# First attention of a ViT tower: norms of queries and keys by four 32-column tiles, one ScalarE copy and a selection matrix

## The reference

```python
q = split_heads(tokens @ Wq, HEADS)            # HEADS, DK, DV = 16, 16, 64
kv = split_heads(tokens @ Wkv, HEADS)
k, v = (kv[..., :DK], kv[..., DK:])
q, k, v = (l2norm(q), l2norm(k), l2norm(v))    # t / max(norm(t), 1e-12)
sim = jnp.einsum('bhid,bhjd->bhij', q, k)
attn = jnp.square(jax.nn.relu(sim))
out = jnp.einsum('bhij,bhjd->bhid', attn, v)
out = tanh_norm(out)                           # tanh(norm) * t / norm
```

## Time and profile before

| what | value |
|---|---|
| median of 3 runs | 3127.56 us (3121.09 to 3130.24) |
| the profiled execution: time, span | 3139.85 us, 3138.1 us |
| mean granted TensorE clock over the span | 0.963 |
| TensorE matmul, busy over the span | 2907.1 us (93%) |
| TensorE weight load, busy over the span | 2217.3 us (71%) |
| VectorE, busy over the span | 2098.8 us (67%) |
| ScalarE, busy over the span | 1442.7 us (46%) |
| GpSimd, busy over the span | 1157.0 us (37%) |

### The profile page before, as it was taken

How to read it: one execution, slowest core, us unless ns; L and a number is a source line. 1 busy time by engine, 2 the same in 40 slices (tenths; PEclk the granted TensorE clock), 3 DMA queues, 4 the chain that set the end, 5 groups by cost and what they waited for, 6 DMA issues and landing times. The chain is left out here.

```text
span 3138.1 us, 66657 instructions
## 1 busy us (share of the span) xinstructions
PE 2907.1 (93%) x21548; PEld 2217.3 (71%) x21549; DVE 2098.8 (67%) x5372; ACT 1442.7 (46%) x2948; POOL 1157.0 (37%) x966
## 2 busy tenths in 40 slices
PE   3899999999999999999966999999999972999998
PEld 1677777777777777777744666666766652999997
DVE  4577677677677777777734777777777855444444
ACT  0444544545545545445422555555555533444443
POOL 3324434434434334334321233333233324444443
PEclk7899999999999999999987999999999985999999
DMA  3424424424424424324302111111111101554544
GB/s 83 96 70 92 107 66 95 107 62 98 102 62 104 98 66 104 94 70 104 87 22 51 49 47 53 43 42 52 45 54 47 44 33 44 77 76 76 77 77 69
DMA packets 161126, 223.12 MB, mean 71 GB/s; under 512 B 30305, under 2 KB 125730, under 8 KB 161074
## 3 DMA queue, kind: packets, MB, share of 16 engines
q1 hardware_dynamic: 135138, 187.50, 23.9%
q0 software_dynamic: 25936, 34.95, 7.2%
HBM read 125.26 MB, written 97.08 MB: 71 GB/s over the span
## 5 line engine op out<-in xcount | busy, mean ns | idle before, releaser
L66 POOL TENSOR_TENSOR vrn<-vsm,inv_root 128x16 f32<-128x16 f32 x64 | 243.8, 3809 | 285.8 <-DVE vsm L836 285.8
L665 ACT ACTIVATE R<-psA 128x1024 f32<-128x1024 f32 x256 | 262.4, 1025 | 168.4 <-PE psA L1150 164.2
L857 DVE TENSOR_TENSOR PR<-R 128x1024 f32<-128x1024 f32 x256 | 321.3, 1255 | 0.0
L2512 POOL DMA_INDIRECT out_rows<-e_y,e_dest x137 | 213.7, 1560 | 289.8 <-DMA out_rows<-e_y,e_dest 182.2
L1904 DVE TENSOR_REDUCE m_nm<-psC 128x4 f32<-128x1028 f32 (+1 forms) x256 | 239.0, 956 | 72.0 <-PE psC L2177 71.4
L1165 PE MATMUL psA<-PR,V 128*64 128x258 f32 x2048 | 283.4, 398 | 0.0
L670 ACT ACTIVATE oTs<-psA 128x258 f32<-128x258 f32 x256 | 99.1, 387 | 358.1 <-PE psA L1165 352.3
L1783 ACT ACTIVATE m_PT<-psC 128x770 f32<-128x770 f32 x256 | 194.0, 810 | 137.3 <-PE psC L2205 137.3
L1210 PE MATMUL psA<-wout,OT 128*128 128x256 f32 x1024 | 244.6, 382 | 0.4 <-DVE OT L899 0.4
L1698 POOL DMA_INDIRECT xg<-tn,idx x124 | 124.5, 1004 | 318.6 <-DMA xg<-tn,idx 186.6
L1210 PEld LDWEIGHTS psA<-wout,OT 128*128 128x128 f32 x1024 | 188.7, 191 | 24.6 <-DVE OT L899 0.7
(11 more groups left out here) (417 smaller groups left out, 7633.0 us busy)
## 6 DMA issues: line engine op xcount, KB each, us to landing
ks<-kparts SPq DMA_DIRECT2D x256, 128.0 KB, 3.3
qs<-qparts SPq DMA_DIRECT2D x256, 128.0 KB, 3.8
e_x<-xg SPq DMA_DIRECT2D x143, 129.0 KB
xraw<-in_x SPq DMA_DIRECT2D x66, 256.0 KB
qparts<-qh SPq DMA_DIRECT2D x128, 128.0 KB, 2.4
kparts<-kh SPq DMA_DIRECT2D x64, 128.0 KB, 2.5
kparts<-kl SPq DMA_DIRECT2D x64, 128.0 KB, 2.4
qparts<-ql SPq DMA_DIRECT2D x64, 128.0 KB, 2.4
```

Of the source, the lines that this page charges most:

```text
L66: return pool.tensor_tensor(out, x, e.to_broadcast(list(out.shape)), ALU.pow)
L665: act.activation(R[:, p % 2].rearrange("p a t n -> p t a n"), ps[:, 0:2, :].rearrange("p t (a n) -> p t a n", a=2), ACT.Relu).then_inc(rel ...
L857: dve.tensor_tensor(PR[:, p % 2, :, :, 0:L], R[:, p % 2], R[:, p % 2], ALU.mult).then_inc(prob_done, 1)
L2512: pool.indirect_dma_start(out, bass.IndirectOffsetOnAxis(ap=dest[:, b % XD:b % XD + 1], axis=0), y[:, b % XD], None, compute_op=ALU.add).t ...
```

## The change

`key_sums` and `query_sums` are taken out. In their place `row_norms` multiplies with the indicator (now 32 columns, 24 of them zero) as the stationary operand and the squares as the moving one, into four tiles of 32 output rows, for both halves of the queries and of the keys. ScalarE copies the 128x256 result to SBUF (`norm_rows`), and `turn_norms` turns it with the selection matrix `sel32` into 32 columns for each half of the tokens. `query_norms` on VectorE moves up to stand right behind `key_norms`.

```diff
+            dve.memset(v.ind8[:, 8:32], 0.0)
+            dve.tensor_copy(v.sel32[:].rearrange("p (g m) -> p g m", g=4),
+                            v.ident[:].rearrange("p (g r) -> p g r", g=4)[:, :, 0:8])
...
+            def norm_rows(j):                       # ScalarE
+                act.wait_ge(norms_summed, j + 1)
+                act.activation(nsums[:], ps[:, BCLS, 0:L], ACT.Copy).then_inc(norms_copied, 1)
...
             def sample (ScalarE)
                     values(j, 1)
+                    norm_rows(j)
                 take_outputs(i, d, 5)
...
             def key_norms(j):                       # VectorE; query_norms likewise
-                dve.wait_ge(kn_done, j + 1)
+                dve.wait_ge(norms_turned, j + 1)
...
             def sample (VectorE)
                     key_norms(j)
+                    query_norms(j, e)
                     tokens(j + 1)
                     value_sums(j, 2)
                     value_sums(j, 3)
                     value_lift(j, 1)
                     value_rows(j, e, 0)
-                    query_norms(j, e)
                     value_rows(j, e, 1)
...
             def mixer_keys(j, t):                   # TensorE
+                if t == 0:
+                    need(pe, racl_done, j)
...
+            def row_norms(j):
+                pe.wait_ge(k_sq, j + 1)
+                pe.wait_ge(q_sq, j + 1)
+                for w, sq in enumerate((qsq, ksq)):
                     for c in range(2):
-                        col = at + 16 * t + 8 * c
-                        last = pe.matmul(ps[:, BCLS, col:col + 8], sq[:, c, t * P:(t + 1) * P], v.ind8[:], start=True,
-                                         stop=True, skip_group_check=True)
+                        g = 2 * w + c
+                        last = pe.matmul(ps[32 * g:32 * g + 32, BCLS, 0:L], v.ind8[:], sq[:, c, :], start=True, stop=True,
+                                         skip_group_check=True)
+                last.then_inc(norms_summed, 1)
+
+            def turn_norms(j):
+                pe.wait_ge(norms_copied, j + 1)
+                for t in range(LT):
+                    col = NORMS + 32 * t
+                    last = pe.matmul(ps[:, BCLS, col:col + 32], nsums[:, t * P:(t + 1) * P], v.sel32[:], start=True,
+                                     stop=True, skip_group_check=True)
+                last.then_inc(norms_turned, 1)
 
             def class_products(j):
-                pe.wait_ge(k_lift, j + 1)
+                pe.wait_ge(q_lift, j + 1)
...
             def sample (TensorE)
                     project_values(j, 1)
+                    row_norms(j)
                 attend(i, d, 5)
                 sim(i, 7)
                 if more:
-                    key_sums(j)
+                    turn_norms(j)
                     project_values(j, 2)
                     project_values(j, 3)
                     class_products(j)
                 attend(i, d, 6)
-                if more:
-                    query_sums(j)
                 attend(i, d, 7)
```

More of the change, by code:

```diff
@@ L416, in mixer_and_attention @@
         osums = sbuf(nc, ctx, "osums", [P, L])
+        nsums = sbuf(nc, ctx, "nsums", [P, L])
         ssb = sbuf(nc, ctx, "ssb", [P, 2, LT, HEADS])
@@ L804, in second_norm, with norms @@
                                       ALU.mult).then_inc(xn_done, 1)
+            def norms(w):
+                return ps[:, BCLS, NORMS:NORMS + 64].rearrange("p (t w g) -> p w t g", t=LT, w=2)[:, w]
             def key_norms(j):
-                dve.wait_ge(kn_done, j + 1)
-                dve.tensor_scalar(km[:], ps[:, BCLS, KN:KN + 32].rearrange("p (t g) -> p t g", t=LT), L2_EPS ** 2, None,
+                dve.wait_ge(norms_turned, j + 1)
+                dve.tensor_scalar(km[:], norms(1), L2_EPS ** 2, None,
                                   ALU.max).then_inc(k_lift, 1)
@@ L844, in query_norms @@
             def query_norms(j, e):
-                dve.wait_ge(qn_done, j + 1)
-                dve.tensor_scalar(qm[:], ps[:, BCLS, QN:QN + 32].rearrange("p (t g) -> p t g", t=LT), L2_EPS ** 2, None,
+                dve.wait_ge(norms_turned, j + 1)
+                dve.tensor_scalar(qm[:], norms(0), L2_EPS ** 2, None,
                                   ALU.max).then_inc(q_lift, 1)
@@ L1112, in project_values @@
                 last.then_inc(v_done, 1)
-            def norm_sums(sq, at):
-                for t in range(LT):
-                    for c in range(2):
-                        col = at + 16 * t + 8 * c
-                        last = pe.matmul(ps[:, BCLS, col:col + 8], sq[:, c, t * P:(t + 1) * P], v.ind8[:], start=True,
-                                         stop=True, skip_group_check=True)
[L1120 to L1124, removed]
+            def row_norms(j):
+                pe.wait_ge(k_sq, j + 1)
+                pe.wait_ge(q_sq, j + 1)
+                for w, sq in enumerate((qsq, ksq)):
+                    for c in range(2):
+                        g = 2 * w + c
[4 more added lines that the diff above has]
+                pe.wait_ge(norms_copied, j + 1)
+                for t in range(LT):
+                    col = NORMS + 32 * t
+                    last = pe.matmul(ps[:, BCLS, col:col + 32], nsums[:, t * P:(t + 1) * P], v.sel32[:], start=True,
+                                     stop=True, skip_group_check=True)
+                last.then_inc(norms_turned, 1)
             def class_products(j):
-                pe.wait_ge(k_lift, j + 1)
+                pe.wait_ge(q_lift, j + 1)
                 for k in range(KT):
@@ L1135, in class_products @@
                 last.then_inc(cls_done, 1)
[L1137 to L1140, removed]
             def sim(i, p):
@@ L2674, in first_weights @@
     v.biasr = sbuf(nc, ctx, "biasr", [P, 768], BF16)
-    v.ind8 = sbuf(nc, ctx, "ind8", [P, 8])
+    v.ind8 = sbuf(nc, ctx, "ind8", [P, 32])
+    v.sel32 = sbuf(nc, ctx, "sel32", [P, 32])
     v.sel8 = sbuf(nc, ctx, "sel8", [P, 8])
```

12 lines of the change are left out of this document (6 added, 6 removed).

## The result

The changed kernel takes 3138.83 us (median of 9 runs, 3136.29 to 3147.97) against 3128.1 us for the kernel before in the same series (9 runs, 3121.09 to 3138.68). The ratio is 1.0035, with a 95% interval from 1.0024 to 1.0047: 0.35% slower, 10.7 us by the medians. The forecast was 8.4 us more.

The account below looks back on a forecast made before the run. A loop through TensorE's work to project_values(j, 3) and a GpSimd chain was taken to bound the kernel. 31 x 0.30 = +9.3, -1.2 for DMA waits, +0.3 for constants: +8.4 us on 3127.56, 3136.0 us; range 3122 to 3144.

Parts of the forecast that it names:

- The loop: First attend, TensorE to project_values(j, 3), square, last sum, GpSimd root, class parts, prob, next first attend: 47.28 us per turn.
- the 30 waits of VectorE for `acl`: At 30 of 31 sample turns VectorE waits for GpSimd's acl before the first prob; read as sign that TensorE doesn't bound.
- TensorE inside the loop: Down to project_values(j, 3): row_norms 0.70 plus turn_norms 0.46 minus key_sums 0.90, +0.26 us per sample (0.23 to 0.32).
- the upper bound of 0.76: row_norms ahead of attend 5: 0.67 us, up to 0.76 if the matmul behind pays 0.09; 0.70 taken.
- 0.30 us: Growth taken per turn: VectorE delays the last value sum by 0.22 to 0.44 us, TensorE by 0.23 to 0.32; larger decides.
- Rival C: VectorE's moved query_norms decides: 0.36 to 0.50 us per turn, +10 to +15 us, around 3140; chance 0.24.
- A: The forecast itself: loop longer by 0.23 to 0.36 us, +6 to +10 us, 3133 to 3138; chance 0.56.
- The covers: ScalarE's copy ends before turn_norms is reached; class_products gets q_lift about when TensorE arrives, and lies outside the loop.
- Where the removed work went: TensorE's stall grows from 0.35 to about 1.3 us, split between sim(i+1, 0) for the DMA and the first attend.
- samples that wait for a late landing: Six later samples wait for the layout DMA anyway, partly covering the longer loop: at most 1.8 us, taken as -1.2.
- B: TensorE bounds the loop after all: all 0.64 us per sample comes back, -19.8 us, 3107.7; chance 0.12.
- D: The layout DMA lands later too: each further 0.1 us costs 3.1 us; with 0.3 us +18 us, 3145; chance 0.08.

Follow-up runs that it names:

- e2: Changed kernel with the four instructions of turn_norms issued twice, 0.43 us more TensorE work inside the loop; ratio 1.0074 to the kernel before.
- e3: Changed kernel with the eight query instructions of class_products issued twice, 0.89 us more TensorE work outside the loop; ratio 1.0041 to the kernel before.
- e4: Kernel before with query_sums cut from eight instructions to two, 0.66 us less TensorE work behind project_values(j, 3); ratio 0.9997.
- e1: Changed kernel run again without any edit; ratio 1.0042 to the kernel before.
- e10: Changed kernel with value chain taken forward, key_norms and query_norms ahead of value_sums(j, 3), each part's store started once written; 3102.21 us, ratio 0.9893 to the kernel before.
- e5: Changed kernel with query_norms behind value_lift(j, 1) on VectorE and class_products behind attend 6 on TensorE; ratio 1.0031 to the kernel before.
- e11: e10 with the old norm_sums for keys and queries instead of four tiles, copy and turn; 3120.18 us, ratio 0.9948 to the kernel before.
- e7: Changed kernel with row_norms behind project_values(j, 2), turn_norms behind project_values(j, 3), class_products behind attend 6, copy and VectorE reordered; ratio 0.9981 to the kernel before.
- e8: Changed kernel with value projections and sums taken forward, query_norms behind prob 7; ratio 0.998 to the kernel before.

## Why the prediction was right

**The loop.** The step on which all rests, that the turn of a sample is set by TensorE's work down to `project_values(j, 3)` and then by a chain over GpSimd, held. e2 and e3 show both sides of it: 13 us of work inside cost 12.1, 28 us outside cost 0.3 in the 31 turns. e4 shows the outer side in the kernel before. In all 31 turns of the kernel before, of the changed one and of e1 to e4, the last value sum starts 0.03 us behind its square.

One of the signs I had read it from proves less than I took it for, the 30 waits of VectorE for `acl`. e10 has the same row, though the turn there is set by TensorE:

```profile
DVE PR L873 <- POOL acl L582: 15.7, 30, 0.6
```

What tells the two apart is the time from `sim` to `attend`. Its shortest at this place is 0.65 us, not the 0.56 of another pair, so the stall in the kernel before was about 0.26 us, not 0.35.

**TensorE inside the loop.** `turn_norms` costs 856.03 - 855.66 = 0.37 us and 0.08 more on the instruction behind (0.31 to the next instead of 0.23), as forecast. `row_norms` was sized at 0.70 and costs 0.77. Its body takes the forecast 0.57 us (853.18 to 853.75), its entry 0.09 (two instructions of line 1125 take 0.55 instead of 2 x 0.23). The rest is the step behind the group, which I had priced at 0.09 in the upper bound of 0.76 and then left out of the 0.70: line 1176 takes 0.32 us to line 1181 (853.75 to 854.07), where in the kernel before the same pair stands 0.21 us apart:

```profile
848.53 0.28 PE L1160 MATMUL psA<-pcl,vcls 80*128 80x258 f32 x1
848.74 1.09 PE L1165 MATMUL psA<-PR,V 128*64 128x258 f32 x8
...
855.66 0.36 PE L1160 MATMUL psA<-pcl,vcls 80*128 80x258 f32 x1
...
855.96 1.09 PE L1165 MATMUL psA<-PR,V 128*64 128x258 f32 x8
```

The second pair of rows, also of the kernel before, stands behind `class_products`, which uses no 32-column tiles, and takes 0.30 us as well; so this step is no price of leaving the tiles. With 0.77 the sum is 0.77 + 0.45 - 0.90 = +0.32 us instead of +0.26; the row for the root says +0.37. The 0.05 that are left I can't attribute to one place: in the medians over the turns they come in steps of 0.01 to 0.02 us at instructions that are the same in both kernels.

**VectorE.** I took 0.30 us by arguing with both engines at once. The runs show that TensorE's part alone decides: the last sum starts 0.03 us behind its square before, after and in e5. Key and query norms together take 0.92 us (858.13 to 859.05), not 0.98, and the sums follow each other after 0.72 us, so VectorE comes just in time. Rival C is excluded, narrowly, and by these rows alone: the time itself, 10.7 us more, lies just above the 6 to 10 us of A, within the 10 to 15 of C.

**The covers.** ScalarE's copy (0.42 us, from 854.26 to 854.68) ended a microsecond before `turn_norms` at 855.66. `class_products` waits 0.17 us on average for `q_lift` (5.1 us, 30 times), outside the loop, as said.

**Where the removed work went.** The stall was forecast to grow to 1.3 us, split between the DMA and the chain. In the sample shown it is 0.24 us at `sim(i+1, 0)` and 821.85 - 820.27 - 0.56 = 1.02 us before `attend`, 1.26 together. Counted from 0.65 us instead of 0.56, this and the forecast are both 0.09 less.

**The sum.** 31 x 0.37 = 11.5 us, and the 31 turns grew by 9.3. I had taken off 1.2 us for samples that wait for a late landing; the traces show something else in that place. In 27 turns the growth is 10.1 us, 0.37 each. The first turn grew by 1.5 (46.00 to 47.52 us). Three turns got shorter, by 2.3 us together: the second, which had a late landing before (48.29 to 47.76), and the 13th and the 30th, which took 48.60 us each before because the clock was halved for 3.4 us in them. So the 8.1 us forecast for the loop came as near to the 9.7 measured as it did with some luck: the growth of a turn was taken too small (0.30 for 0.37), and two stretches of half clock in the one trace of the kernel before make up for it in part. The 0.3 us for the constants aren't seen: the first `attend` starts at 106.5 us, before at 106.7. The medians differ by 10.7 us.

**The rivals.** B, TensorE's total work: out by e3 and e4. D, a later landing: out, the wait for the DMA became longer because TensorE came earlier (`sim(i+1, 0)` starts 863.69 - 821.85 = 41.84 us behind the first `attend`, before 859.21 - 817.30 = 41.91), and the next first `attend` still follows `acl` by 2.33 us as before.

## What to carry to other kernels

In a hand-pipelined loop, look for the closed path from one turn to the next and ask of each edit on which side of it the work lies; work moved from outside to inside costs time though the total shrinks. An engine that a window shows 99% busy can have a stall at every turn; a change that shortens it there is worth nothing until the chain and the transfer that end last with it are moved first, and then it is worth nearly its full instruction time (e10 against e11: ratios of 0.9893 and 0.9948 to the kernel before). When an operation is moved, look for who waits for it: three of my reorderings (e5, e7, e8) lost gain to a wait of `class_products` for `query_norms`, which had been moved back. And when a number comes out as expected, look whether the path is the expected one too: in e5 and e7 it was not.

## What the runs showed of the hardware that I had not expected

GpSimd's root of 128x16 values takes 3.80 us when VectorE's `value_rows` has started just before it (VectorE at 861.03 for 1.22 us, GpSimd at 861.20), and 2.89 us when the root starts first (e5: GpSimd at 863.42, VectorE at 863.74). The first root shows it within the change itself; the first row is of the kernel before, where `prob(i, d, 7)` had VectorE as the root began, the second of the changed kernel, where the root came first:

```profile
851.69 3.99 POOL L66 TENSOR_TENSOR vrn<-vsm,inv_root 128x16 f32<-128x16 f32 x1 [8.16 <-DVE vsm L836]
856.24 2.90 POOL L66 TENSOR_TENSOR vrn<-vsm,inv_root 128x16 f32<-128x16 f32 x1 [8.18 <-DVE vsm L849]
```

In 31 samples that is 31 x 1.09 = 34 us, about the 31.4 us less of GpSimd on the page, and it was worth nothing here: it lengthens GpSimd's idle time before the second root (0.21 to 1.52 us), which the last sum releases. The 0.91 us between the two second roots are about what was left of VectorE's instruction (1.05 us). In e5 to e10 the second root had been put ahead in this way by a by-product of the new order, which is part of why the chain over GpSimd is no longer the wall there; how much of the gain it makes was not measured by itself. What makes the root wait is inferred from the order of the starts; no run changes that order alone.

Around the group in the 32-column tiles, which itself takes 0.57 us, TensorE spends 0.09 us more before it and 0.11 us more behind it (the latter as behind `class_products` without such tiles), so that four matmuls in four tiles cost 0.77 us where four of the old way cost 0.90; the saving of the change comes mostly from covering keys and queries with one group instead of two.
